# GRU and expert layer on one core: first expert products of steps 0 and 1 in column groups, six whole-array ones a block

## The chip, the cores and the metric

The kernel runs on one core of a Trainium2 chip. The metric is the device time of one execution in microseconds. Beside it stands one profiled execution, whose trace gives the start and the length of every instruction on TensorE (PE; its weight loads are listed apart as PEld), VectorE (DVE), ScalarE (ACT), GpSimd (POOL) and SyncE (SP, which issues the transfers).

## What is computed

A GRU runs over 256 time steps for 16 sequences of width 512, and its states go through a layer of eight low-rank experts, of which the two best of each state are mixed and added to the input:

```python
def cell(h, x):
    gi = x @ W_ih + b_ih
    gh = h @ W_hh + b_hh
    i_r, i_z, i_n = jnp.split(gi, 3, axis=-1)
    h_r, h_z, h_n = jnp.split(gh, 3, axis=-1)
    r = jax.nn.sigmoid(i_r + h_r)
    z = jax.nn.sigmoid(i_z + h_z)
    n = jnp.tanh(i_n + r * h_n)
    h_new = (1.0 - z) * n + z * h
    return (h_new, h_new)
...
    router_logits = x / norm @ router_w
    routing_weights = jax.nn.softmax(router_logits.astype(jnp.float32), axis=-1)
    rw, selected_experts = jax.lax.top_k(routing_weights, TOP_K)
    rw = rw / jnp.sum(rw, axis=-1, keepdims=True)
...
    for e in range(N_EXPERTS):
        out = out + combine[:, e, None] * (x @ Wa[e] @ Wb[e])
```

Here the layer's x is the GRU's states, `Wa[e]` is 512 x 128 and `Wb[e]` 128 x 512, and the whole function returns the input plus the layer's output.

## The kernel before

The recurrence is the backbone: step n needs the state of step n - 1. Eight steps make a block (S = 8; 8 steps x 16 sequences are 128 tokens), and there are 32 blocks (T = 256). Below, step s is n % 8. Every fp32 product is made of three fp16 ones (`TERMS`: high x high, high x low, low x high); a product whose stationary operand is still in the array skips its load (`matmul_held`, L843), others go by L852.

**TensorE.** A step begins with `state_part`: the state times the recurrent weights into the banks `gates` (L932 and L937) and `zbank`. These have 32 stationary columns and go to four column groups of the array, four matmuls side by side. The rest of a step is work that does not hang on the newest state:

- `pair_part`: the input products of two steps ahead into a bank `pairs`, in 12 units of four column-group matmuls with 384 moving columns. `UNITS` says how many an odd step does; the next even step does the rest.
- `expert_down`, the **first product** of expert e for a block: 12 matmuls with the whole array (128 stationary columns of `wa`, 128 tokens moving) into one of two `ybank`s.
- `expert_up_by_tokens`, the **second product**: three slots of four column-group matmuls (32 tokens stationary, 512 columns of `wb` moving) into `nbank` or `obank`.
- `route` in step 3: the router's logits of the block before, whole-array.

Expert e of block f has the number m = 8 f + e. `DOWN[e]` and `UP[e]` say how many steps after its block's first step the products are issued, so DOWN % 8 is the step's place in a block:

```python
DOWN = (9, 9, 11, 11, 13, 13, 15, 15)
UP = (12, 12, 14, 14, 16, 16, 18, 18)
UNITS = (12, 5, 12, 3, 12, 5, 12, 5)
...
for n in range(1, T):
    state_part(n)
    if n % 2:
        wide_step(n)
    else:
        grouped_step(n)
```

A wide step issues two first products (behind the router in step 3) and then its units; a grouped step its units and then two second products. The last twelve experts and the last block's first products are in `last_experts`.

**VectorE** carries the recurrence: it transposes `gates` (`tr`, L734), sums, makes `npre`, `u` and at last the new state `st` (L765), on which the next `gates` products wait. Behind that it does one `add_expert` a step (L801, expert m = n - 12) and in steps 0, 2, 5 and 6 a transpose of `gi_n` (L772). **ScalarE** does the sigmoids and the tanh, seeds `gates` and `zbank` from `pairs` (L570, L577), and in `beside` the rest: `split_y` (two copies of a first product, high part L645 and fp32 L649), `gather_states` for the router (L625, both halves in step 0), the bias copy, in the first 17 steps one weight split a step (L547). **GpSimd** subtracts to get a product's low part (`low_y`, L459) and does small things for the router. Both follow `downs_at`. SP's transfers are issued by step and none of them is touched.

Of the kernel before, what the change touches and what calls it, by code (L numbers as in the profile page):

```python
# [23 lines left out]
def wait(eng, sem, value):  # L24
    if value > 0:
        eng.wait_ge(sem, value)


def gru_moe_kernel(nc, x, cond, W_ih, W_hh, b_ih, b_hh, router_w, Wa, Wb, out):
# [4 lines left out]
    NB = T // S  # L34


    DOWN = (9, 9, 11, 11, 13, 13, 15, 15)
    UP = (12, 12, 14, 14, 16, 16, 18, 18)
    UNITS = (12, 5, 12, 3, 12, 5, 12, 5)
    ADD = S + 4  # L40
    YB = 6

# [10 lines left out]
    with ExitStack() as ctx:  # L53
# [106 lines left out]

        def downs_at(n):

            return [n - DOWN[e] + e for e in range(NE) if DOWN[e] % S == n % S and n >= DOWN[e]]

        def ups_at(n):
            return [n - UP[e] + e for e in range(NE) if UP[e] % S == n % S and n >= UP[e]]

# [3 lines left out]
        def y_at(m):  # L171
            return ybanks[m % 2]
# [228 lines left out]
        def _(pool):  # L401
# [100 lines left out]
            def beside(n):  # L502
                i, s = n // S, n % S
                if s == 0 and 1 <= i:
                    fold_squares(i - 1)
                    add_squares(i - 1)
                if s in (1, 2) and 1 <= i:
                    less_upper_half(i - 1, s - 1)
                if s == 3 and 1 <= i:
                    invert_norm(i - 1)  # L510
                if s == 4 and 1 <= i:
                    combine(i - 1)
                if s in (4, 6) and 1 <= i and i + 2 < NB:
                    split_x(i + 2, s // 6, n)
                for m in downs_at(n):
                    low_y(m)
                if s == 3 and 1 <= i:
                    gaps(i - 1)
# [19 lines left out]
        def _(act):  # L538
# [83 lines left out]
            def gather_states(f, part):  # L622
                act.wait_ge(both_parts_ready, 2 * ((f + 1) * S + 1))
                wait(act, logits_done, f)
                nc.scalar.activation(hf[:, part, :, :].rearrange("p k (s b) -> p (k s) b", b=B),  # L625
                                     hparts[:, f % HB, :, :, part * B:(part + 1) * B].rearrange(
                                         "p k s b -> p (k s) b"), ACT.Copy).then_inc(hf_ready, 1)
# [23 lines left out]
            def beside(n):  # L651
                i, s = n // S, n % S
                if s % 2 == 0 and n + 4 < T:
                    put_biases(n // 2 + 2)
                for m in downs_at(n):
                    split_y(m)
                if s == 7:
                    square(i)
                if s == 0 and 1 <= i:
                    for part in range(2):  # L660
                        gather_states(i - 1, part)
                if s == SPLIT_AT and i + 3 < NB:
                    split_x(i + 3)
                if s == SCALE_AT and 1 <= i and i + 2 < NB:
                    scale_x(i + 2)
                if n == 0:
                    split_first(2)
                if 0 <= n < len(SPLITS) - N_GRU_SPLITS:
                    split_weights(N_GRU_SPLITS + n)
# [170 lines left out]
        def _(pe):  # L840
# [8 lines left out]
            def product(held, out, lhsT, rhs, start, stop, cols=P, col0=0):  # L849
                if held:  # L850
                    return matmul_held(out, lhsT, rhs, cols, col0, start, stop)
                return nc.tensor.matmul(out, lhsT, rhs, start=start, stop=stop, skip_group_check=True)  # L852
# [96 lines left out]
            def route(f):  # L949
                bank = router_bank(f)  # L950

                if f == 0:
                    pe.wait_ge(weights_split, splits_before(N_RW_SPLITS))

                if f == NB - 1:
                    pe.wait_ge(acc_done, LEFT - 1)
                else:
                    pe.wait_ge(yhi_ready, f * NE + 2)
                    pe.wait_ge(y32_ready, f * NE + 2)

                wait(pe, router_read, f)
                pe.wait_ge(sq_step, (f + 1) * SQ_STEPS)
                for part in range(3):
                    nc.tensor.matmul(bank[:, P + NE:P + NE + 1], upper_half(part), ones_bf[:, :],
                                     start=(part == 0), stop=(part == 2), skip_group_check=True)
                pe.wait_ge(hf_ready, 2 * (f + 1))
                n = 0
                for k in range(K):
                    for ph, pw in TERMS:
                        mm = product((ph, pw) == (0, 1), bank[:, P:P + NE], hf[:, ph, k, :], rw[:, pw, k, :], n == 0,  # L970
                                     n == 3 * K - 1)
                        n += 1
                mm.then_inc(logits_done, 1)

            def wait_first_product(m):
                f, e = m // NE, m % NE

                wait(pe, yhi_ready, m - 1)
                wait(pe, y32_ready, m - 1)
                if e == 3 and f < NB - 1:  # L980
                    pe.wait_ge(router_read, f + 1)
                if e == 0:
                    pe.wait_ge(both_parts_ready, 2 * ((f + 1) * S + 1))
                if m in wa_split_at:
                    pe.wait_ge(weights_split, splits_before(wa_split_at[m]))

            def expert_down(m):
                f, e = m // NE, m % NE
                wait_first_product(m)
                n = 0  # L990
                for k in range(K):
                    for pw, ph in TERMS:
                        mm = product((pw, ph) == (0, 1), y_at(m)[:, 0:P], wa[:, pw, k, e, :],
                                     hparts[:, f % HB, k, :, ph * B:(ph + 1) * B], n == 0, n == 3 * K - 1)
                        n += 1
                mm.then_inc(y_done, 1)

# [36 lines left out]
            def pair_ahead(n):  # L1034

                s, p, all_units = n % S, (n + AHEAD) // 2, K * len(TERMS)
                if n % 2 and n > 1 and UNITS[s - 1] < all_units:
                    pair_part(p - 1, range(UNITS[s - 1], all_units))
                if p < T // 2:
                    pair_part(p, range(UNITS[s]) if n % 2 else range(UNITS[s - 1] if n else 6, UNITS[s] if n else all_units))  # L1040

# [7 lines left out]

            def grouped_step(n):  # L1050
                pair_ahead(n)
                for m in ups_at(n):
                    expert_up_by_tokens(m)
                if n == 0:
                    turn_first(2)

# [29 lines left out]
            grouped_step(0)  # L1086
            for n in range(1, T):
                state_part(n)
                if n % 2:
                    wide_step(n)  # L1090
                else:
                    grouped_step(n)
# [23 lines left out]
```

## Time and profile before

| what | value |
|---|---|
| median of 3 runs | 1017.51 us (1017.07 to 1017.79) |
| the profiled execution | 1017.07 us |
| its span, first to last instruction | 1015.3 us |
| PE busy | 979.9 us (97%) |
| DVE busy | 876.0 us (86%) |
| ACT busy | 694.6 us (68%) |
| POOL busy | 291.3 us (29%) |
| granted TensorE clock | 0.998 |

The span covers the execution but for 1.8 us around it. Matmuls of the four column groups overlap, so a slot of four counts once, and PE's busy time is that of a pipeline with modelled ends; what a slot costs is read from the distance between starts. A timeline row gives the start in us, the length, the engine, line and operation, the tile written and those read, the count of merged instructions, and in brackets the idle time before it and who ended it.

### The profile page before, as it was taken

How to read it: one execution, taken by the hardware profiler on the slowest of the kernel's cores; microseconds unless marked ns; L12 is line 12 of the kernel's file. 1: busy time of each engine (PE TensorE's matmuls, PEld its weight loads, DVE VectorE, ACT ScalarE, POOL GpSimd, SP SyncE). 2: the span in 40 equal slices, each digit the busy share in tenths (PEclk: the TensorE clock that was granted, in tenths of full speed). 3: DMA queues.
4: the chain of work that ended last, by engine and by line, in shares of the span. 5: the costliest groups of instructions: out<-in, count | busy, mean ns of one | idle time of the engine just before them, and what ended most of it. 6: DMA issues, size and time to landing. Idle time of an engine off the chain costs nothing.

```text
span 1015.3 us, 60728 instructions
## 1 busy us (share of the span) xinstructions
PE 979.9 (97%) x29067; PEld 669.2 (66%) x20799; DVE 876.0 (86%) x3631; ACT 694.6 (68%) x2696; POOL 291.3 (29%) x729
## 2 busy tenths in 40 slices
PE   4789999999999999999999999999999999999997
PEld 2456667667667666766667676676666676666664
DVE  6889888888888888888888888888888888888886
ACT  6687766776666677676677666667766667776663
POOL 1032323322323332322332233332223333223223
PEclk9999999999999999999999999999999999999999
DMA  8221111111111111111101111111111111110000
GB/s 301 87 81 31 29 32 30 30 28 33 27 32 33 28 26 35 27 32 32 30 24 35 30 30 30 32 26 32 29 29 33 30 24 33 30 30 19 15 9 28
DMA packets 49360, 38.83 MB, mean 38 GB/s; under 512 B 34532, under 2 KB 38972, under 8 KB 49084
## 3 DMA queue, kind: packets, MB, share of 16 engines
q1 hardware_dynamic: 48236, 31.41, 11.5%
q8 instruction: 198, 3.24, 1.4%
q10 hardware_dynamic: 848, 3.54, 1.0%
q14 instruction: 78, 0.64, 0.2%
HBM read 18.94 MB, written 8.39 MB: 27 GB/s over the span
## 4 chain that ended last, share of the span: by engine, by line
PE 89%; DVE 6%; ACT 2%; DMA 1%; issue 1%; ACTq 0%; DVEq 0%; POOL 0%; POOLq 0%
PE pairs L852 16%; PE ybank L852 12%; PE gates L932 11%; PE gates L937 11%; PE pairs L843 7%; PE ybank L843 6%; PE zbank L843 5%; PE zbank L852 5%; PE obank L852 5%; PE nbank L852 5%; PE obank L843 3%; PE nbank L843 2%; DMA wih<-in_L_cond_W_ih 1%; DVE acc L801 1%; DVE tr L734 1%
## 5 line engine op out<-in xcount | busy, mean ns | idle before, releaser
L852 PE MATMUL pairs<-wx,xs 128*32 128x384 f16 x4096 | 281.1, 328 | 1.2 <-DVE wx L714 1.2
L598 ACT ACTIVATE rr<-pre 128x64 f32<-128x64 f32 x256 | 65.7, 257 | 240.4 <-DVE pre L737 240.4
L852 PE MATMUL ybank<-hparts,wa 128*128 128x128 f16 x2048 | 193.9, 219 | 0.0
L459 POOL TENSOR_TENSOR y<-y 128x128 f16<-128x128 f32 x256 | 106.3, 436 | 258.8 <-ACT y L649 250.9
L852 PEld LDWEIGHTS ybank<-hparts,wa 128*128 128x128 f16 x2048 | 159.8, 98 | 29.5 <-issue 16.0
L843 PE MATMUL ybank<-hparts,wa 128*128 128x128 f16 x1024 | 178.2, 219 | 0.0
L843 PE MATMUL pairs<-wx,xs 128*32 128x384 f16 x2048 | 174.3, 326 | 0.0
L932 PE MATMUL gates<-whh,st 128*32 128x256 f16 x4080 | 157.3, 273 | 15.7 <-DVE st L765 15.5
L852 PEld LDWEIGHTS pairs<-wx,xs 128*32 128x32 f16 x4096 | 108.4, 97 | 95.9 <-issue 54.6
L932 PEld LDWEIGHTS gates<-whh,st 128*32 128x32 f16 x4080 | 103.5, 96 | 85.3 <-ACT gates L570 63.3
L937 PE MATMUL gates<-whh,hparts 128*32 128x256 f16 x4080 | 157.5, 273 | 0.0
L852 PE MATMUL zbank<-whh,hparts 128*32 128x128 f16 x4080 | 145.8, 219 | 0.0
L843 PE MATMUL zbank<-whh,hparts 128*32 128x128 f16 x4080 | 145.7, 219 | 0.0
L734 DVE STREAM_TRANSPOSE tr<-gates 128x256 f32<-128x256 f32 x256 | 114.6, 448 | 28.7 <-PE gates L937 20.7
L852 PEld LDWEIGHTS zbank<-whh,hparts 128*32 128x32 f16 x4080 | 114.3, 97 | 14.2
L937 PEld LDWEIGHTS gates<-whh,hparts 128*32 128x32 f16 x4080 | 111.9, 97 | 1.0
L570 ACT ACTIVATE gates<-pairs,step_rows 128x256 f32<-128x256 f32 x256 | 110.1, 430 | 0.1
L761 DVE SCALAR_TENSOR_TENSOR u<-nn,omz 128x64 f32<-128x64 f32 x256 | 57.7, 225 | 51.4 <-ACT nn L610 51.4
L606 ACT ACTIVATE zz<-pre 128x64 f32<-128x64 f32 x256 | 65.7, 257 | 50.8 <-DVE pre L745 47.2
L852 PE MATMUL obank<-wb,y 128*32 128x512 f16 (+1 forms) x980 | 98.2, 379 | 0.0
L852 PE MATMUL nbank<-wb,y 128*32 128x512 f16 x976 | 96.7, 379 | 0.0
L577 ACT ACTIVATE zbank<-pairs,step_rows 128x128 f32<-128x128 f32 x256 | 85.0, 332 | 0.0
(134 smaller groups left out, 1817.3 us busy)
## 6 DMA issues: line engine op xcount, KB each, us to landing
out<-outb SPq DMA_DIRECT2D x63, 128.0 KB
xin<-in_x SPq DMA_DIRECT2D x58, 128.0 KB
wih<-in_L_cond_W_ih ACTq DMA_DIRECT2D x4, 768.0 KB, 7.8
whh<-in_L_cond_W_hh SPq DMA_DIRECT2D x4, 768.0 KB, 12.0
wih<-in_L_ffn_Wb SPq DMA_DIRECT2D x8, 256.0 KB, 2.7
xs<-xh SPq DMA_TRANSPOSE x116, 3.0
wih<-in_L_ffn_Wa SPq DMA_DIRECT2D x4, 256.0 KB, 4.3
whh<-in_L_ffn_Wa SPq DMA_DIRECT2D x4, 256.0 KB, 3.0
```

What stands on the lines that cost most here:

```text
L459: nc.gpsimd.tensor_tensor(y[:, m % YB, 1, :], y32[:, m % 2, :], y[:, m % YB, 0, :], ALU.subtract).then_inc(ylo_ready, 1)
L570: nc.scalar.activation(gates[:, 0:2 * P], pairs[n // 2 % 2][:, 0:2 * P], ACT.Copy, scale=step_rows[:, q:q + 1]).then_inc(seeded, 1)
L577: nc.scalar.activation(zbank[:, 0:P], pairs[n // 2 % 2][:, 2 * P:3 * P], ACT.Copy, scale=step_rows[:, q:q + 1]).then_inc(z_seeded, 1)
L598: nc.scalar.activation(rr[:, :], pre[:, RG, :, :].rearrange("p k b -> p (k b)"), ACT.Sigmoid, scale=1 / PROD_SCALE).then_inc(r_ready, 1)
L606: nc.scalar.activation(zz[:, :, :].rearrange("p k b -> p (k b)"), zpre, ACT.Sigmoid, scale=1 / PROD_SCALE).then_inc(z_ready, 1)
L734: nc.vector.transpose(tr[:, 0:2 * K, :].rearrange("p (g k) c -> p g k c", k=K), gates[:, 0:2 * P].rearrange("p (g c k) -> p g k c", g=2, k ...
L761: nc.vector.scalar_tensor_tensor(out=u[:, :], in0=nn[:, :], scalar=PART_SCALE, in1=omz[:, :], op0=ALU.mult, op1=ALU.mult).then_inc(u_ready, 1)
L801: nc.vector.scalar_tensor_tensor(out=(outb if e == NE - 1 else acc)[:, :], in0=o_at(m)[:, :], scalar=comb[:, e:e + 1], in1=(xin[:, f % XIN ...
L843: return nc.tensor.add_instruction(mybir.InstMatmult(name=nc.get_next_instruction_name(), engine=mybir.EngineType.PE, start_tensor_calc=start,
L852: return nc.tensor.matmul(out, lhsT, rhs, start=start, stop=stop, skip_group_check=True)
L932: nc.tensor.matmul(gates[32 * j:32 * j + 32, 0:2 * P], st[:, k, :], whh[:, 1, k, j, 0:2 * P], start=False, stop=False, skip_group_check=True)
L937: mm = nc.tensor.matmul(gates[32 * j:32 * j + 32, 0:2 * P], prior[:, k, :], whh[:, 0, k, j, 0:2 * P], start=False, stop=(k == K - 1), skip ...
```

## The change

`DOWN` is now (11, 11, 13, 13, 15, 15, 16, 17): two first products each in steps 3, 5 and 7, and one each in steps 0 and 1 of the next block. `UP` has expert 5 a step later, so that steps 0 and 1 have one second product each. Step 1 is no wide step any more: steps 0 and 1 go through `grouped_step`, which issues the units, then a first product in column groups (`expert_down_by_ranks`: each of the 12 matmuls becomes four, with 32 of the 128 columns of `wa` each), then the second product. `UNITS` gives step 1 six units and step 2 the other six. Of the two gathers for the router one is in step 0 and one in step 1. GpSimd takes both low parts of steps 0 and 1 in step 1. For the last block's end, four first products are put into steps 254 and 255, whole-array.

```diff
-    DOWN = (9, 9, 11, 11, 13, 13, 15, 15)
-    UP = (12, 12, 14, 14, 16, 16, 18, 18)
-    UNITS = (12, 5, 12, 3, 12, 5, 12, 5)
+    DOWN = (11, 11, 13, 13, 15, 15, 16, 17)
+    UP = (12, 12, 14, 14, 16, 17, 18, 18)
+    UNITS = (12, 6, 12, 3, 12, 5, 12, 5)
...
         def downs_at(n):
 
+            if n >= T - 2:
+                return [LEFT + 2 * (n - T + 2), LEFT + 2 * (n - T + 2) + 1]
             return [n - DOWN[e] + e for e in range(NE) if DOWN[e] % S == n % S and n >= DOWN[e]]
...
-                for m in downs_at(n):
+                for m in (downs_at(n - 1) + downs_at(n) if s == 1 else [] if s == 0 else downs_at(n)):
                     low_y(m)
...
-                if s == 0 and 1 <= i:
-                    for part in range(2):
-                        gather_states(i - 1, part)
+                if s in (0, 1) and 1 <= i:
+                    gather_states(i - 1, s)
...
-                    pe.wait_ge(yhi_ready, f * NE + 2)
-                    pe.wait_ge(y32_ready, f * NE + 2)
+                    wait(pe, yhi_ready, f * NE)
+                    wait(pe, y32_ready, f * NE)
...
-                if e == 3 and f < NB - 1:
+                if e == 1 and f < NB - 1:
                     pe.wait_ge(router_read, f + 1)
...
+            def expert_down_by_ranks(m):
+                f, e = m // NE, m % NE
+                wait_first_product(m)
+                n = 0
+                for k in range(K):
+                    for pw, ph in TERMS:
+                        for g in range(4):
+                            of = slice(32 * g, 32 * g + 32)
+                            mm = product((pw, ph) == (0, 1), y_at(m)[of, 0:P], wa[:, pw, k, e, of],
+                                         hparts[:, f % HB, k, :, ph * B:(ph + 1) * B], n == 0, n == 3 * K - 1, 32, 32 * g)
+                        n += 1
+                mm.then_inc(y_done, 1)
...
             def grouped_step(n):
                 pair_ahead(n)
+                if n < T - 2:
+                    for m in downs_at(n):
+                        expert_down_by_ranks(m)
                 for m in ups_at(n):
                     expert_up_by_tokens(m)
+                if n == T - 2:
+                    for m in downs_at(n):
+                        expert_down(m)
...
-                if n % 2:
+                if n % S in (3, 5, 7):
                     wide_step(n)
```

TensorE, step 0 of a steady block, from its first input units (`pairs`) to its end; `ybank` rows are first products, `nbank` and `obank` rows second ones. Before:

```order
L852 MATMUL pairs<-wx,xs 32x384 x8
L843 MATMUL pairs<-wx,xs 32x384 x4
L852 MATMUL pairs<-wx,xs 32x384 x8
L843 MATMUL pairs<-wx,xs 32x384 x4
L852 MATMUL pairs<-wx,xs 32x384 x4
L852 MATMUL nbank<-wb,y 32x512 x4
L843 MATMUL nbank<-wb,y 32x512 x4
L852 MATMUL nbank<-wb,y 32x512 x4
L852 MATMUL obank<-wb,y 32x512 x4
L843 MATMUL obank<-wb,y 32x512 x4
L852 MATMUL obank<-wb,y 32x512 x4
```

And now, from the last input unit on:

```order
L853 MATMUL pairs<-wx,xs 32x384 x4
L853 MATMUL ybank<-hparts,wa 32x128 x4
L844 MATMUL ybank<-hparts,wa 32x128 x4
L853 MATMUL ybank<-hparts,wa 32x128 x8
L844 MATMUL ybank<-hparts,wa 32x128 x4
L853 MATMUL ybank<-hparts,wa 32x128 x8
L844 MATMUL ybank<-hparts,wa 32x128 x4
L853 MATMUL ybank<-hparts,wa 32x128 x8
L844 MATMUL ybank<-hparts,wa 32x128 x4
L853 MATMUL ybank<-hparts,wa 32x128 x4
L853 MATMUL nbank<-wb,y 32x512 x4
L844 MATMUL nbank<-wb,y 32x512 x4
```

The second of the two second products has left the step, and 48 matmuls of a grouped first product have come between the units and the other one.

TensorE, step 1 of a steady block, from the last `zbank` slot to the first units. Before, there are 24 whole-array matmuls between them:

```order
L843 MATMUL zbank<-whh,hparts 32x128 x4
L852 MATMUL ybank<-hparts,wa 128x128
L843 MATMUL ybank<-hparts,wa 128x128
L852 MATMUL ybank<-hparts,wa 128x128 x2
L843 MATMUL ybank<-hparts,wa 128x128
```

Now the units come first, and the step stays in column groups to its end:

```order
L844 MATMUL zbank<-whh,hparts 32x128 x4
L853 MATMUL pairs<-wx,xs 32x384 x4
L844 MATMUL pairs<-wx,xs 32x384 x4
L853 MATMUL pairs<-wx,xs 32x384 x8
L844 MATMUL pairs<-wx,xs 32x384 x4
L853 MATMUL pairs<-wx,xs 32x384 x4
L853 MATMUL ybank<-hparts,wa 32x128 x4
L844 MATMUL ybank<-hparts,wa 32x128 x4
```

Six units stand where five stood behind the whole-array products, and the first product is a grouped one behind them.

## Rows read from the trace of the kernel before

**Rows 1.** The page: shares of the chain; a group of loads (busy us, mean ns)

```profile
PE 89%; DVE 6%; ACT 2%; DMA 1%; issue 1%; ACTq 0%; DVEq 0%; POOL 0%; POOLq 0%
...
L852 PEld LDWEIGHTS pairs<-wx,xs 128*32 128x32 f16 x4096 | 108.4, 97 | 95.9 <-issue 54.6
```

**Rows 2.** Timeline of PE, steps 0 to 2 of a steady block: start us, length us, what

```profile
572.81 0.62 PE L932 MATMUL gates<-whh,st 128*32 128x256 f16 x16
...
574.13 0.51 PE L852 MATMUL pairs<-wx,xs 128*32 128x384 f16 x8
...
575.27 0.40 PE L852 MATMUL nbank<-wb,y 128*32 128x512 f16 x4
...
576.56 0.62 PE L932 MATMUL gates<-whh,st 128*32 128x256 f16 x16
...
577.44 0.24 PE L852 MATMUL zbank<-whh,hparts 128*32 128x128 f16 x4
...
577.83 0.24 PE L843 MATMUL zbank<-whh,hparts 128*32 128x128 f16 x4
578.00 0.23 PE L852 MATMUL ybank<-hparts,wa 128*128 128x128 f16 x1
...
579.30 0.22 PE L852 MATMUL ybank<-hparts,wa 128*128 128x128 f16 x1
579.45 0.35 PE L852 MATMUL pairs<-wx,xs 128*32 128x384 f16 x4
...
580.11 0.34 PE L843 MATMUL pairs<-wx,xs 128*32 128x384 f16 x4
580.30 0.62 PE L932 MATMUL gates<-whh,st 128*32 128x256 f16 x16
...
584.05 0.41 PE L932 MATMUL gates<-whh,st 128*32 128x256 f16 x8
```

**Rows 3.** Timeline of PE, first block: starts of steps 2, 3 and 4

```profile
32.98 0.62 PE L932 MATMUL gates<-whh,st 128*32 128x256 f16 x16 [1.40 <-DVE st L765]
...
36.63 0.62 PE L932 MATMUL gates<-whh,st 128*32 128x256 f16 x16 [1.01 <-DVE st L765]
...
40.35 0.62 PE L932 MATMUL gates<-whh,st 128*32 128x256 f16 x16 [1.73 <-DVE st L765]
```

**Rows 4.** Timeline of PE, last block: starts of steps 254 and 255

```profile
989.52 0.62 PE L932 MATMUL gates<-whh,st 128*32 128x256 f16 x16 [0.70 <-DVE st L765]
...
993.23 0.62 PE L932 MATMUL gates<-whh,st 128*32 128x256 f16 x16 [0.92 <-DVE st L765]
```

**Rows 5.** Timeline of DVE, the stretch of rows 2: tr, st, one expert add

```profile
573.92 0.45 DVE L734 STREAM_TRANSPOSE tr<-gates 128x256 f32<-128x256 f32 x1 [0.19 <-PE gates L937]
...
576.09 0.23 DVE L765 TENSOR_TENSOR st<-u,v 128x64 f16<-128x64 f32 x1
...
576.86 0.71 DVE L801 SCALAR_TENSOR_TENSOR acc<-nbank,comb,acc 128x512 f32<-128x512 f32 x1
577.67 0.45 DVE L734 STREAM_TRANSPOSE tr<-gates 128x256 f32<-128x256 f32 x1
...
579.92 0.23 DVE L765 TENSOR_TENSOR st<-u,v 128x64 f16<-128x64 f32 x1
```

**Rows 6.** Timeline of PEld (weight loads), the same stretch

```profile
577.33 0.51 PEld L852 LDWEIGHTS zbank<-whh,hparts 128*32 128x32 f16 x16
...
581.56 0.18 PEld L852 LDWEIGHTS pairs<-wx,xs 128*32 128x32 f16 x8
```

**Rows 7.** Timelines of PE and ACT, steps 8 and 9

```profile
58.73 0.62 PE L932 MATMUL gates<-whh,st 128*32 128x256 f16 x16 [1.00 <-DVE st L765]
...
62.60 0.62 PE L932 MATMUL gates<-whh,st 128*32 128x256 f16 x16
...
59.20 1.13 ACT L625 ACTIVATE hf<-hparts 128x512 f16<-128x512 f16 x2
```

**Rows 8.** Timeline of POOL, the low parts of step 7's first products

```profile
573.42 0.82 POOL L459 TENSOR_TENSOR y<-y 128x128 f16<-128x128 f32 x2 [3.28 <-ACT y L649]
```

## Prediction

> **What bounds the kernel now.** I read first the shares of the chain that ended last, for the whole execution, then TensorE's timeline over three steps of a steady block, then VectorE's over the same stretch, then stretches in which TensorE has too little to do. TensorE holds 89% of it [rows 1], but that hides two different kinds of step. A step begins with its first `gates` product. Steps 0, 1 and 2 of this block begin at 572.81, 576.56 and 580.30, and step 3 at 584.05 [rows 2]: 3.75, 3.74 and 3.75 us. In step 0 the last expert product runs straight into the next `gates` (1.32 us of state products, seven input units in 1.14 us, so 0.163 each, six groups of second products in 1.29 us, so 0.215 each): TensorE sets that step. In step 1 the last unit starts at 580.11 and would be through at 580.27, yet `gates` starts at 580.30: there the recurrence sets the end, by 0.03 us.
>
> How fast the recurrence can go is seen where TensorE idles. In the first block, which has no experts, steps 2 and 3 take 36.63 - 32.98 = 3.65 and 40.35 - 36.63 = 3.72 us, with idle times of about a microsecond and more before `gates`, each released by VectorE's `st` [rows 3]. Near the end, with VectorE adding experts as usual, step 254 takes 993.23 - 989.52 = 3.71 us [rows 4]. VectorE's rows give the pieces [rows 5]: `gates` begins about 1.1 us ahead of `tr` (576.56 to 577.67), `tr` to `st` takes 576.09 - 573.92 = 2.17 us in step 0 and 579.92 - 577.67 = 2.25 in step 1 (the odd step has one more semaphore wait in it), and the next `gates` starts 0.38 after `st` when it is waited for. So no even step can be under about 3.65 us, no odd one under about 3.72. Step 5 escapes the extra wait, and nothing is changed there.
>
> **The transitions.** In step 1 the last of the column-group products (`zbank`) starts at 577.83; groups of that kind start 0.056 apart ((577.83 - 577.44) / 7), yet the first whole-array product starts at 578.00, 0.17 later. The last whole-array one starts at 579.30 and the column groups go on at 579.45, 0.15 later [rows 2]. Against 0.056 that is 0.11 and 0.09 lost; with slower first intervals on each side a whole-array stage costs 0.22 to 0.24 us beside its products. There are four such stages in a block, and three after the change.
>
> **The change, part by part.** The array time of a first product does not change by itself. Whole, 24 matmuls for two experts take 24 slots of 0.056, 1.34 us. In column groups one expert is 12 slots of four matmuls with 128 moving columns, the shape of the `zbank` slots, which also take 0.056: 12 x 0.056 = 0.67 us. This form with `wa` is not in the trace. Its lower bound is these 0.67 us (the moving columns are the same number, so nothing makes it less). Its upper bound is from the loads: the `zbank` slots come with 16 weight loads in 8 slots, 0.445 us, or 27.8 ns a load; a grouped first product has 32 loads in 12 slots, and if 27.8 ns were the pace of a load it would take 0.89 us. I take 0.67, because elsewhere eight loads of the same 32-column form are together over in 0.18 us, though one lasts 97 ns by itself [rows 1, 6]: they overlap across the column groups and start 10 ns apart or closer, while 0.67 / 32 = 21 ns is needed.
>
> The Trainium skill speaks against that choice. "TensorE: Matmul & The Clock Gate", section on LDWEIGHTS, gives a load's time as its columns divided by 1.2 ns, which for 32 columns is 26.7 ns, and "TensorEngine Tiling (Array Packing)", Gotcha 2, says that column tiling excludes fast weight load. An estimate by these pages, with the loads one behind the other, is 0.85 us a product, and the sum below would come out near 1022.5 us.
>
> The steps then need of TensorE:
> - Step 0: 1.32 + 1.14 + 0.67 + one second product 0.645 = 3.78 us (was 3.75). TensorE sets it.
> - Step 1: 1.32 + six units 0.98 + 0.67 + 0.645 = 3.61. The recurrence needs 3.72, so it takes 3.72 (was 3.74), with TensorE idle for 0.11.
> - Step 2: 1.32 + 0.98 + 1.29 = 3.59. The recurrence needs 3.65 (was 3.75), idle 0.06.
> - Steps 3 to 7 issue the same on TensorE: two whole-array first products in 3, 5 and 7, two second products in 4 and 6.
>
> Together 11.15 us against 11.24 in this block [rows 2], and against 11.23 by the middle of all 29 blocks: about 0.08 a block. That is the point of the sum: of the 0.22 us and more taken off TensorE two thirds turn into waiting for `st`. Steps 0 to 2 of the blocks 3 to 31 are of this kind, 29 x 0.08 = **2.3 us gained**.
>
> At the start, step 9 takes 62.60 - 58.73 = 3.87 where 3.72 is possible. ScalarE gathers both halves of `hf` (1.13 us) ahead of a weight split in step 8 and comes late to the next sigmoid [rows 7]. The change puts one half into step 9, and takes the first products and their copies out of it; step 10 loses their low parts beside its own sums. I put twice the 0.15 us of step 9, **0.3 us gained**, between 0 and 0.35. In steps 13 to 18 VectorE carries weight splits and expert adds together; nothing of that moves, 0.
>
> At the end, step 254 now has two whole-array first products behind its two second products: 1.32 + 1.29 + 1.34 + about 0.2 of transitions = 4.15 to 4.17, where the recurrence took 3.71 [rows 4]. **0.45 us lost**, and nothing later gets it back, since everything that follows hangs on the last state.
>
> Costs put at nothing. The two y copies of an expert move on ScalarE (two from step 1 to step 0, one gather the other way); both steps leave it idle before the next sigmoid. The two GpSimd subtractions stay in step 1. The lead of a second product over its first shrinks from three steps to one, but a pair whose first products were in step 7 has its low parts by 573.42 + 0.82 = 574.24 us [rows 8], and an even step asks for the first of them 2.46 us into itself (575.27 in step 0 [rows 2]), a microsecond later; only step 4 has its first products 0.4 us later in the step before, behind the router, and it asks 0.33 us later too. The last second product of step 0 now ends with the step: a slot lasts 0.40 us and the next starts 0.215 after it, so its end is 0.18 after the next `gates` starts; VectorE's add starts 0.3 after it (576.86 against 576.56 [rows 2, 5]), so the margin is a few hundredths to a tenth. If that cover fails the add slips by as much, and has 0.1 us more before `tr`. No DMA moves.
>
> Sum: -2.3 - 0.3 + 0.45 = -2.15 us. The profiled execution took 1017.07 us against a median of 1017.51; taken off the median this gives **1015.3 us**. A measurement of this kernel can tell about 0.2% (2.0 us) from no change, and the forecast stands right on that edge.
>
> **The rivals.**
> - *The loads set the pace* (slower than before). At 27.8 ns a load the product takes 0.89 us; step 0 becomes 4.00, step 1 3.83, step 2 stays at 3.65: 11.48, 0.24 more than before, x 29 = +7.0, and with start and end 1024.6 us. It turns the sign from about 0.75 us a product, since step 1 hides 0.11 us but step 0 nothing. For it: exactly 27 to 28 ns a load is what `zbank` and `gates` slots have. Against: the eight loads in 0.18 us [rows 6]. The skill's rule is this rival, at 1022.5. Chance 0.13.
> - *The gain drowns.* Some 0.04 to 0.08 us a block are lost in step 0 (a bubble where the grouped product meets its semaphores) or in step 2, which has no slack at all any more, so that any lateness of VectorE counts there: 29 x 0.08 gone leaves +0.15, 1016.5 to 1018 us. Chance 0.22.
> - *The recurrence is no floor here.* Then the whole 0.22 to 0.24 us a block comes through, less the 0.45 at the end: 29 x 0.23 = 6.7, so 1017.51 - 6.7 - 0.3 + 0.45 = 1011.0 us; with half of it 1014.3. Against it: the 0.03 us of idle already seen in step 1. Chance 0.15.
>
> **How the numbers follow.** The forecast has 0.50, with 1014.3 to 1016.4 as its own range; some six tenths of it lie beyond 0.2%. Faster: 0.30 + 0.15 and a little of the second rival, 0.46. Within 0.2%: 0.39. Slower: 0.15. The range leaves out the deepest part of the third rival and the full price of the first: 1013 to 1020 us.
>
> **What would show it.** Right: steps 0, 1 and 2 of a steady block of 3.78, 3.72 and 3.65 us; twelve slots of `ybank` in 0.67 us with no jump at either side; idle time before `gates` put down to `st` of 0.11 us after step 1 and 0.06 after step 2, in all some 5 us more than before; step 254 at 4.15. Wrong: slots of `ybank` over 0.062 us, a `gates` in step 2 that starts later than 0.38 after `st`, or a VectorE add that waits for TensorE.

## The result and the profile after

| | before | after |
|---|---|---|
| median, 12 runs each on one chip | 1017.28 us (1016.47 to 1017.96) | 1019.18 us (1018.64 to 1020.68) |
| profiled execution: time, span | 1017.07, 1015.3 us | 1019.46, 1017.7 us |

The ratio is 1.0019, with an interval of 1.0012 to 1.0027: the change costs about 1.9 us, where 2.15 us of gain were forecast. The lines of the page that differ, first of the kernel before:

```profile
PE 979.9 (97%) x29067; PEld 669.2 (66%) x20799; DVE 876.0 (86%) x3631; ACT 694.6 (68%) x2696; POOL 291.3 (29%) x729
...
q8 instruction: 198, 3.24, 1.4%
```

and of the changed kernel:

```profile
PE 980.1 (96%) x31227; PEld 676.3 (66%) x22239; DVE 876.5 (86%) x3631; ACT 695.6 (68%) x2696; POOL 291.6 (29%) x729
...
q8 instruction: 212, 3.47, 1.4%
PE 89%; DVE 6%; ACT 2%; DMA 1%; issue 1%; ACTq 0%; DVEq 0%; POOL 0%; POOLq 0%
```

TensorE is busy for as long as before, and the chain has the shares of [rows 1], though the span is 2.4 us longer. What changed are the counts: 2160 matmuls and 1440 loads more (60 grouped products by 36 and 24). The queue that brings instructions carried 14 more packets of 16 KB, and 3600 / 256 = 14.06. TensorE's semaphore instructions count too: with the some 960 that each trace records it has 50830 instructions before and 54429 after, and divided by 256 that is 198.6 and 212.6, for 198 and 212 packets. A packet is 256 TensorE instructions, in every run below as well.

The three steps that the prediction rested on, in the stretch that answers to [rows 2]; timeline of PE in the changed kernel, start and length in us:

```profile
574.44 0.62 PE L933 MATMUL gates<-whh,st 128*32 128x256 f16 x16
...
576.73 0.35 PE L853 MATMUL pairs<-wx,xs 128*32 128x384 f16 x4
576.89 0.24 PE L853 MATMUL ybank<-hparts,wa 128*32 128x128 f16 x4
...
577.51 0.24 PE L853 MATMUL ybank<-hparts,wa 128*32 128x128 f16 x4
577.56 0.40 PE L853 MATMUL nbank<-wb,y 128*32 128x512 f16 x4
...
578.21 0.62 PE L933 MATMUL gates<-whh,st 128*32 128x256 f16 x16
...
581.94 0.62 PE L933 MATMUL gates<-whh,st 128*32 128x256 f16 x16
```

Step 0 takes 578.21 - 574.44 = 3.77 us and step 1 takes 3.73. The twelve `ybank` slots take 577.56 - 576.89 = 0.67 us, with no jump at either side. From the starts of `gates` in blocks 3 to 30 the middle lengths of steps 0, 1 and 2 are 3.772, 3.731 and 3.651 us (before 3.749, 3.731 and 3.749), and steps 3 to 7 are as they were. That is 0.075 us a block gained, as forecast. Step 24 starts at 118.37 (before 118.56), 0.19 gained. The gain is there in nearly every block, and yet the kernel is slower.

The rest is in single steps. Adding up by how much each step from 24 to 252 exceeds the middle length of its place in the block gives 1.7 us before and 6.0 us after. In the kernel before these are nearly all five VectorE operations that start some 0.35 us late, in steps 48, 63, 178, 193 and 239; the other kernels have them too (e4 all but the one in step 48). The new ones are on TensorE. Timeline of PE around one in step 57:

```profile
244.24 0.40 PE L853 MATMUL nbank<-wb,y 128*32 128x512 f16 x4
244.46 0.41 PE L933 MATMUL gates<-whh,st 128*32 128x256 f16 x8
245.42 0.40 PE L933 MATMUL gates<-whh,st 128*32 128x256 f16 x8 [0.56 <-issue]
245.63 0.62 PE L938 MATMUL gates<-whh,hparts 128*32 128x256 f16 x16
```

PEld over the same stretch:

```profile
244.31 0.36 PEld L933 LDWEIGHTS gates<-whh,st 128*32 128x32 f16 x9 [0.16 <-ACT gates L572]
245.42 0.12 PEld L933 LDWEIGHTS gates<-whh,st 128*32 128x32 f16 x7 [0.76 <-issue]
```

Matmuls and loads stop together in the middle of `gates`, where nothing waits on a semaphore, and the idle time is put down to "issue": to nothing that the profile shows. The ninth matmul starts 0.83 us after the eighth, 0.74 later than its place in the row of slots, and step 57 is longer by 0.74 us. The waits of the whole execution show it: before, `tr` waited for `gates` 93 times, 20.7 us in all and 0.4 at the longest; after,

```profile
DVE tr L735 <- PE gates L938: 24.5, 96, 1.1
```

There are seven such stops between steps 24 and 252, of 0.33 to 1.01 us in steps 34, 43, 57, 105, 162, 209 and 233, with one of 0.29 in step 81 and smaller ones beside them. The eight together are 4.3 us, which is what the excess has grown by. Numbering all of TensorE's records in the trace from 0 (matmuls, loads and its semaphore instructions, in the order of their starts), **every one of the seven stands ahead of a record whose number leaves 193 when divided by 256**. The transfers around the stop in step 57 (from 242.0 to 244.2 us):

```profile
q1 hardware_dynamic: 230, 0.05, 11.6%
q8 instruction: 1, 0.02, 4.8%
```

4.8% of 16 engines over 2.2 us is one packet of 1.69 us. By the list of transfers it started at 242.31 and ended at 244.00, and the next instruction ran at 245.42, 1.42 later. For the six others of these stops the distance from the packet's end to the next instruction is 1.4 to 1.7 us. So the theory taken into the experiments, **F**: TensorE reaches the end of its 256 instructions before the next 256 are there, because with a grouped first product (80 instructions for 0.67 us of work, where a whole-array one has 20) a step has some 260 instructions instead of 200. Its rivals: **W**, the stops are waits for other engines that the new order brings; **L**, the grouped loads are slow somewhere; **C**, only the number of packets counts, however they are spread.

### The profile page after: what moved, and what is told of

Read it like the earlier page. It is cut to its first block, busy times and chain, and to the rows that moved or that the text cites. A ratio compares the mean times of both kernels' runs of the same rounds, so it can differ in the third digit from the quotient of the medians.

```text
span 1017.7 us, 64327 instructions
## 1 busy us (share of the span) xinstructions
PE 980.1 (96%) x31227; PEld 676.3 (66%) x22239; DVE 876.5 (86%) x3631; ACT 695.6 (68%) x2696; POOL 291.6 (29%) x729
## 3 DMA queue, kind: packets, MB, share of 16 engines
q8 instruction: 212, 3.47, 1.4%
## 4 chain that ended last, share of the span: by engine, by line
PE 89%; DVE 6%; ACT 2%; DMA 1%; issue 1%; ACTq 0%; DVEq 0%; POOL 0%; POOLq 0%
PE pairs L853 16%; PE ybank L853 12%; PE gates L933 12%; PE gates L938 11%; PE pairs L844 7%; PE ybank L844 6%; PE zbank L853 5%; PE zbank L844 5%; PE obank L853 5%; PE nbank L853 5%; PE nbank L844 2%; PE obank L844 2%; DMA wih<-in_L_cond_W_ih 1%; DVE tr L735 1%; DVE acc L802 1%
## 5 line engine op out<-in xcount | busy, mean ns | idle before, releaser
L853 PE MATMUL pairs<-wx,xs 128*32 128x384 f16 x4096 | 287.3, 328 | 0.9 <-DVE wx L715 0.9
L853 PE MATMUL ybank<-hparts,wa 128*32 128x128 f16 (+1 forms) x3488 | 200.0, 219 | 0.0
L853 PEld LDWEIGHTS ybank<-hparts,wa 128*32 128x32 f16 (+1 forms) x3488 | 167.1, 97 | 30.9 <-issue 12.0
L844 PE MATMUL ybank<-hparts,wa 128*128 128x128 f16 (+1 forms) x1744 | 181.2, 219 | 0.4 <-issue 0.4
L844 PE MATMUL pairs<-wx,xs 128*32 128x384 f16 x2048 | 176.4, 327 | 0.0
L853 PEld LDWEIGHTS pairs<-wx,xs 128*32 128x32 f16 x4096 | 113.1, 97 | 95.1 <-issue 53.6
L933 PE MATMUL gates<-whh,st 128*32 128x256 f16 x4080 | 158.5, 273 | 16.9 <-DVE st L766 16.1
```

Source lines behind the costliest of these rows:

```text
L844: return nc.tensor.add_instruction(mybir.InstMatmult(name=nc.get_next_instruction_name(), engine=mybir.EngineType.PE, start_tensor_calc=start,
L933: nc.tensor.matmul(gates[32 * j:32 * j + 32, 0:2 * P], st[:, k, :], whh[:, 1, k, j, 0:2 * P], start=False, stop=False, skip_group_check=True)
```

## Experiments

**e1_quarter: the changed kernel without three quarters of the grouped products.** It leaves out ranks 32 to 127 of experts 6 and 7 in blocks 0 to 29, so its time is that of less work.

```diff
-                        for g in range(4):
+                        for g in range(1):
```

> The changed kernel, but a grouped first product issues only the matmuls of its first column group: 12 matmuls and 8 loads instead of 48 and 32, the same 12 slots of array time, the same mode, the same waits. It leaves out ranks 32 to 127 of experts 6 and 7 (4 to 7's last blocks aside). Theory F (the steady steps got faster as forecast, but the denser instruction stream of steps 0 and 1 outruns TensorE's instruction fetch at some of the 256-instruction boundaries): the pauses before instructions number 193 + 256 k go, the middle step lengths stay at 3.77, 3.73 and 3.65, and the time is about 4 us under the changed kernel, near 1015 us, below the kernel before. Rival W (the pauses are waits for other engines, which the new places of the products bring): the waits are the same, so the time stays at 1019 us. Rival L (weight loads set the pace somewhere): it would fall too, but the slots of ybank would get shorter than 0.056 us.

Measured: 1015.32 us, ratio 0.9983 (0.9974 to 0.9992). The page:

```profile
PE 977.9 (97%) x29067; PEld 676.7 (67%) x20799; DVE 874.9 (86%) x3631; ACT 695.0 (69%) x2696; POOL 294.8 (29%) x729
...
q8 instruction: 198, 3.24, 1.3%
```

The count of matmuls and loads is exactly that of before, the packets too, and of the stops one of 0.30 us is left; excess over middle lengths 2.1 us. Single steps did not come as expected (steps 0 and 1 take 3.654 and 3.838: three of the four matmuls of the second product's first slot start some 0.2 us ahead of the first product's last one, which shortens step 0, and in step 1 VectorE's add comes late and puts off `tr` by 0.11), but steps 0 to 2 together take 11.14 against 11.15 in the changed kernel. With the same gain and without the stops it is 1.65 us faster than the kernel before measured beside it (1016.97 us), where 2.15 were forecast; that its time is the forecast 1015.3 to the digit is chance. It takes loads away too, so by itself it does not tell F from L.

**e2_dense_before: the kernel before with more instructions for the same columns.** In steps 0 and 1 every unit is cut in three matmuls of 128 columns, the second and third with their weights held: 56 and 40 instructions more.

```diff
+                    for c in (range(3) if cut else (None,)):
+                        to, of = (slice(P, 4 * P), slice(0, 3 * P)) if c is None else (
+                            slice((c + 1) * P, (c + 2) * P), slice(c * P, (c + 1) * P))
```

> The kernel before, with nothing moved, but from step 24 on each 384-column matmul of the input units of steps 0 and 1 is cut into three of 128 columns with the same weights held: 56 more instructions in step 0 and 40 in step 1, no load more. Array time by slots of 0.056 against 0.163: 0.005 us a unit, 0.03 a block that counts, 1.0 to 1.2 us in all. Theory F: pauses appear at instruction boundaries as in the changed kernel, 2 to 5 us on top, so 1020 to 1023 us. Rival W: no pauses, 1018.3 us.

Measured: 1019.82 us, ratio 1.0025 (1.0014 to 1.0036), between W's 1018.3 and F's 1020 to 1023; q8 has 209 packets (2784 / 256 = 10.9 more). It is slower, with no grouped product, no load and no wait added. Only part is F's: stops at the 193rd record are 0.48 us in step 226 and 0.25 in step 148; the middle length of step 0 grew by 0.035 (1 us in all); and in this execution the first step began 0.58 us later. So a small weight for F by itself, against W and L.

**e3_padded: the changed kernel with 64 idle matmuls and their loads ahead of everything.**

```diff
+            for _ in range(64):
+                nc.tensor.matmul(gates[:, 0:P], zeros, zeros, start=True, stop=True, skip_group_check=True)
```

> The changed kernel with 64 idle matmuls and their 64 loads ahead of everything else on TensorE, while it would wait for the first transfers: 128 instructions, half a block of 256. Theory F: the pauses stay at numbers 193 + 256 k of the instructions as recorded and so move to other steps; their sum is of the same size, 3 to 6 us, and the time within 2 us of 1019. Rival W: the pauses stay in the same steps as in the changed kernel (34, 43, 57, 81, 105, 162, 233) and move away from 193 + 256 k to 65 + 256 k.

Measured: 1018.66 us, ratio 1.0017 (1.0006 to 1.0027), excess 6.1 us, as large as without the shift. (The profiled execution is the longest of the ten, 1022.08 us; its first step began 2.7 us later than the changed kernel's.) No step of the changed kernel's list has its stop again: step 57 runs through, and the long stops are now in steps 41, 121, 145, 146, 169, 211, 235 and 250 (0.26 to 0.86 us). All eight stand again ahead of records that leave 193. The first of them, timeline of PE:

```profile
188.01 0.24 PE L853 MATMUL ybank<-hparts,wa 128*32 128x128 f16 x4
188.06 0.40 PE L853 MATMUL obank<-wb,y 128*32 128x512 f16 x3
188.86 0.39 PE L853 MATMUL obank<-wb,y 128*32 128x512 f16 x1 [0.40 <-issue]
```

The stop cuts a slot of four matmuls after the third. A wait of the program would move with the step; this one stays at a count of instructions. That is the clearest evidence for F, and it excludes W; L has no place for it either, since no load of the steps was changed.

**e4_halves: the grouped product in two groups of 64 columns**, 24 matmuls and 16 loads.

```diff
-                        for g in range(4):
-                            of = slice(32 * g, 32 * g + 32)
+                        for g in range(2):
+                            of = slice(64 * g, 64 * g + 64)
```

> The changed kernel with a grouped first product in two groups of 64 columns: 24 matmuls and 16 loads instead of 48 and 32. If column groups of 64 stand beside those of 32 without a transition, the array time is the same, half of the added instructions are gone and with them the pauses: 1015 to 1016 us. If 64 columns are a mode of their own, each such product pays 0.2 us of transitions as a whole-array stage does: step 0 becomes 3.99 and step 1 3.83, 0.33 us a block more, so 1019.2 - 4 + 9.6 = 1025 us.

Measured: 1025.86 us, ratio 1.0085 (1.0072 to 1.0099). No stop is left (excess 2.0 us, 203 packets), but steps 0 and 1 take 4.020 and 3.847. Timeline of PE, step 0:

```profile
579.18 0.35 PE L853 MATMUL pairs<-wx,xs 128*32 128x384 f16 x4
579.46 0.25 PE L853 MATMUL ybank<-hparts,wa 128*64 128x128 f16 x2
...
580.10 0.22 PE L853 MATMUL ybank<-hparts,wa 128*64 128x128 f16 x2
580.25 0.40 PE L853 MATMUL nbank<-wb,y 128*32 128x512 f16 x4
```

After a unit the next slot of the same form comes 0.163 later, here 0.28; and behind the product 0.15 in place of 0.056. Groups of 64 columns beside groups of 32 pay about what a whole-array stage pays. So fewer instructions took the stops away, and the transitions cost more than the stops had.

**e5_spread: the grouped products in steps 0 and 2, with step 1 sparse between them.** `DOWN` and `UP` are changed, the end is as in the kernel before.

```diff
+    DOWN = (8, 10, 11, 11, 13, 13, 15, 15)
+    UP = (12, 12, 14, 14, 16, 17, 17, 18)
```

> Same number of grouped first products and of transitions as in the changed kernel, but the two dense steps stand apart: DOWN = (8, 10, 11, 11, 13, 13, 15, 15), so the grouped ones are in steps 0 and 2, UP = (12, 12, 14, 14, 16, 17, 17, 18), so step 1 has two second products, and nothing is added at the end. Steps 0, 1 and 2: 3.78, 3.73 and 3.65, 0.07 a block less than before, 2.0 us, and 0.2 at the start. Theory F with the density within one block of 256 instructions as what decides: a fetch boundary now seldom finds a full block in a dense stretch, the pauses shrink to 1 us or less, and the time is 1015 to 1016.5 us, under both kernels. If instead only the number of instructions counts, it is 1018 to 1019 us.

Measured: 1021.5 us, ratio 1.005 (1.0036 to 1.0064), excess 7.6 us, middle lengths 3.772, 3.729, 3.649: a miss. A sparse step between two dense ones does not help. The longest stop, in step 138 at the 193rd record, is in the middle of a slot of the grouped product:

```profile
554.28 0.22 PE L842 MATMUL ybank<-hparts,wa 128*32 128x128 f16 x1
555.09 0.22 PE L842 MATMUL ybank<-hparts,wa 128*32 128x128 f16 x3 [0.60 <-issue]
```

A step of 260 instructions is longer than a packet: one that falls within it is used up in the step alone, whatever its neighbour does. That covers six of this kernel's ten stops over 0.25 us. The other four, the longest among them, ended packets that took 4.3 to 4.6 us; what sets them apart is told below the table.

**e6_both_in_1: both grouped products in step 1**, which then has 312 instructions (112 + 40 + 160; the recorded text has 304) (`DOWN` and `UP` of the kernel before, six units).

```diff
+    DOWN = (9, 9, 11, 11, 13, 13, 15, 15)
+    UP = (12, 12, 14, 14, 16, 16, 18, 18)
```

> DOWN and UP of the kernel before, but the two first products of step 1 are grouped ones, with six units in steps 1 and 2 each: 304 instructions in step 1. Medians: step 0 3.75, step 1 3.72 (needs 3.64), step 2 3.65: 0.10 a block, 2.9 us less than before, no cost at the end. Theory F: this is the densest stream of all, 256 instructions in about 2.7 us, so pauses are longer, 0.5 us and more wherever a boundary falls there, and eat the gain: 1017 to 1021 us. Rival W: 1014 us.

Measured: 1025.6 us, ratio 1.0087 (1.0073 to 1.01), worse than expected. Middle lengths hardly move (3.749, 3.735, 3.669), and the excess is 15.5 us: 24 stops of 0.3 to 1.0 us, all at the 193rd record. The profiled execution is the longest of the five. The waits of this kernel:

```profile
DVE tr L733 <- PE gates L936: 31.9, 92, 1.2
```

The count of packets is 213, as in e5 and e8 below, and the excess twice theirs: C falls, how fast a packet is used up does count.

**e7_units5: the changed kernel with five units in step 1 and seven in step 2**, to see whether the state sets the length of steps 1 and 2.

```diff
-    UNITS = (12, 6, 12, 3, 12, 5, 12, 5)
+    UNITS = (12, 5, 12, 3, 12, 5, 12, 5)
```

> The changed kernel with five units in step 1 and seven in step 2. If the recurrence is the floor as forecast, step 1 stays at 3.73 though TensorE has 0.16 us less to do, and step 2 goes from 3.65 to 3.75, so 0.10 a block, 2.9 us more, with somewhat fewer pauses: 1020 to 1022 us. If there is no such floor the two steps together stay at 7.38 and the time at 1019 us.

Measured: 1021.22 us, ratio 1.0042 (1.0028 to 1.0056). Timeline of PE, steps 1 and 2:

```profile
578.84 0.62 PE L933 MATMUL gates<-whh,st 128*32 128x256 f16 x16
...
582.57 0.62 PE L933 MATMUL gates<-whh,st 128*32 128x256 f16 x16
...
586.32 0.62 PE L933 MATMUL gates<-whh,st 128*32 128x256 f16 x16
```

Step 1 keeps its 3.73 us with 0.163 us less to do; step 2, which has that unit more, goes from 3.65 to 3.75. So the recurrence is the floor of step 1, and step 2 had 0.06 us above TensorE's need.

**e8_tail: the changed kernel with step 254's two first products in column groups.**

```diff
-                if n < T - 2:
-                    for m in downs_at(n):
-                        expert_down_by_ranks(m)
+                for m in downs_at(n):
+                    expert_down_by_ranks(m)
...
-                if n == T - 2:
-                    for m in downs_at(n):
-                        expert_down(m)
```

> The changed kernel with the two first products of step 254 grouped instead of whole-array. Step 254 becomes 1.32 + 1.29 + 1.34 = 3.95 instead of 4.15: 0.2 us less, which the times can't tell from nothing; the trace can.

Measured: 1019.37 us, ratio 1.0022 (1.0013 to 1.0031). Step 254 takes 3.95 in place of 4.18, the transitions' 0.22. The program is otherwise that of the changed kernel, and the stops are mostly in its steps again (34, 57, 105, 162, 209 and 233 among them) with other lengths (step 57 1.10, step 105 0.88): the places are fixed by the program, the lengths vary from execution to execution. The excess is 7.2 us (steps 24 to 252 alone), against 6.0 in the changed kernel with the same instructions there: that much can differ between two executions.

**e9_woven and e10_bunched: the changed kernel's instructions of steps 0 and 1 in other orders.** By then F was held in a sharper form: what counts is how fast the last 190 or so instructions ahead of the end of a packet run. Both kernels have the same instructions a step; one weaves slots of units (U), the grouped first product (Y) and the second product (P), the other puts the first product right ahead of the next `gates`.

```diff
+    ORDER = {0: "UYYYUUYYUYPPYYYUUYYYUP", 1: "UUUYYUUYYYYPPYYUPYYYY"}
```

```diff
+    ORDER = {0: "UUUUUUUPPPYYYYYYYYYYYY", 1: "UUUUUUPPPYYYYYYYYYYYY"}
```

> The changed kernel with the same instructions in steps 0 and 1 in another order (blocks 3 to 30): units, slots of the grouped first product and slots of the second product take turns, so that the 80 short instructions of the first product are spread over the step. Counts, tile forms and step lengths stay. Theory F (pauses come where TensorE runs through the some 190 instructions ahead of a 256 boundary faster than a block is fetched): the fastest 190 consecutive records of the changed kernel take 2.33 us; here by slot lengths 2.6 us. Steps 0, 1, 2 keep their middle lengths of 3.77, 3.73 and 3.65; the excess over middle lengths falls from 6.0 to 2.5 to 4.5 us; time 1016.0 to 1018.0 us. Theory C (only the number of fetched blocks counts, 212 as in the changed kernel): excess near 6, 1019.2 us. If the turns between banks cost something by themselves, step 0 gets longer than 3.80 and time goes above 1020.

> The changed kernel with the same instructions in steps 0 and 1, but units first, then the second product, then the grouped first product right ahead of the next gates (blocks 3 to 30). The 80 short instructions then stand against the 112 of gates and zbank: by slot lengths the fastest 190 consecutive records take 2.0 us in place of 2.33. Theory F: more and longer pauses, excess 8 to 13 us, time 1021 to 1026 us, middle lengths as in the changed kernel. Theory C (number of fetched blocks, unchanged): 1019.2 us.

Measured: 1019.15 us, ratio 1.002 (1.0011 to 1.0029), excess 5.6 us; and 1018.91 us, ratio 1.0018 (1.0009 to 1.0027), excess 5.1 us. Both miss. In e9 the weaving brought the fastest 190 records from 2.33 to 2.43 us only, not to 2.6, so it is a weak test; in e10 they take 1.90, and neither the time nor the excess went up. Even the stop of step 57 stays where it was. Timeline of PE of e10, where other work stands ahead of it:

```profile
243.59 0.24 PE L854 MATMUL ybank<-hparts,wa 128*32 128x128 f16 x4
243.65 0.41 PE L934 MATMUL gates<-whh,st 128*32 128x256 f16 x8
244.47 0.40 PE L934 MATMUL gates<-whh,st 128*32 128x256 f16 x8 [0.42 <-issue]
```

More telling is the time in which a whole packet is used up, from one 193rd record to the last one ahead of the next (stretches between 118.5 and 985 us, one execution of each kernel; stops counted behind stretches of every length; excess as above; a stop of 0.25 to 0.3 can be mostly the usual wait for the state):

| kernel | packets (q8) | fastest stretch of 256, us | stretches under 4.0 us | stops over 0.25 us at a 193rd record | excess, us |
|---|---|---|---|---|---|
| before | 198 | 4.26 | 0 | 0 | 1.7 |
| e4_halves | 203 | 4.19 | 0 | 0 | 2.0 |
| e1_quarter | 198 | 4.21 | 0 | 1 | 2.1 |
| e2_dense_before | 209 | 3.51 | 27 | 1 | 3.2 |
| e7_units5 | 212 | 3.48 | 51 | 6 | 4.0 |
| e10_bunched | 212 | 3.60 | 52 | 8 | 5.1 |
| e9_woven | 212 | 3.50 | 51 | 7 | 5.6 |
| after | 212 | 3.49 | 51 | 8 | 6.0 |
| e3_padded | 213 | 3.49 | 52 | 8 | 6.1 |
| e8_tail | 213 | 3.48 | 51 | 12 | 7.2 |
| e5_spread | 213 | 3.47 | 47 | 10 | 7.6 |
| e6_both_in_1 | 213 | 2.58 | 31 (26 under 3.5) | 24 | 15.5 |

A step of 3.73 us with some 256 instructions uses a packet up in a step however they are ordered, which fits that e9 and e10 changed nothing, and e5 nothing for the better.

The length of the stretch alone does not decide it. The list of transfers, taken together with the records, does. The twelve traces have 2240 such stretches and 85 stops. Where the next packet's transfer ended 1.5 us or more ahead of the last record of the packet in use (2072 times), there is no stop; where it ended less than 1.1 us ahead of it (67 times), there is one 66 times. From the end of a transfer to the first record of its packet it is never under 1.15 us, and 1.2 to 1.8 at the stops. No transfer began more than 0.8 us ahead of the first record of the packet before it. So a stop is what three times have over the stretch: from the previous 193rd record to the start of the transfer, the transfer itself, and about 1.4 us behind it. Of the 85 stops 17 ended stretches of 4.0 to 5.4 us, and there the transfer had begun 1.6 to 3.7 us after the previous 193rd record; the longest of e5 is one (3.19 us late in a stretch of 4.58).

## Why the prediction was wrong

- *The transitions, the grouped product, the steps.* Right. The first product takes 0.67 us in groups; steps 0, 1 and 2 take 3.77, 3.73 and 3.65 (forecast 3.78, 3.72, 3.65); e4 shows the transition once more as 0.1 us on each side. Over 29 blocks 2.2 us came in. One sign did not show where it was looked for: TensorE's waits on `st` are 16.1 us in all, against 15.5 before, not some 5 us more, because a row of 0.40 us reaches over so short a gap. The starts show it: from the last slot to the next `gates` it is 0.31 us after step 1 and 0.26 after step 2, where a slot takes 0.215, so 0.10 and 0.04 us idle against 0.11 and 0.06 forecast.
- *The floor.* Right: e7 moved a unit and step 1 stayed at 3.73. The rival without a floor is out.
- *The loads set the pace.* Out. 32 loads in 0.67 us are 21 ns each. (The eight loads of [rows 6] start 11 ns apart in the mean, not 10 or closer, which changes nothing.) The Trainium skill's time of a load in "TensorE: Matmul & The Clock Gate", section on LDWEIGHTS, taken for one load behind the other, would give 0.85 us; this trace does not agree, with loads that take turns over four column groups.
- *The start.* The sign right, the size off: 0.19 us gained where 0.3 was put. Step 9 came down from 3.87 to 3.82 only, step 10 from 3.93 to 3.78.
- *The end.* Right: step 254 takes 995.60 - 991.42 = 4.18 us (forecast 4.15 to 4.17; 3.71 before), 0.46 us lost.
- ***Costs put at nothing.*** **This is the step that failed.** It went through copies, subtractions, semaphores and transfers of the program, and "No DMA moves" was true of those alone. The 60 instructions that a grouped product has beside a whole-array one were counted as array time and as loads, never as instructions that have to be brought. What the runs showed in its place is that TensorE stops for 0.3 to 1.0 us where a packet of 256 instructions is used up before the next is there. That put 4.3 us on the account (6.0 less 1.7): -2.2 - 0.2 + 0.46 + 4.3 = 2.36, against 2.4 between the two spans (1.9 between the medians).
- *The rivals.* "The gain drowns" had the right form, a bubble in dense steps, but was priced at no more than the gain, and as a small loss in each block. It is none in most blocks and half a microsecond or more in a few. The only rival on the slower side was the one on loads. The range of 1013 to 1020 still holds the measured time, but by luck: it was drawn for other rivals than the one that came.

The Trainium skill has the mechanism and speaks against its mattering: "Runtime: NRT & Kernel Launch", section "Instruction fetch mechanics", says that instructions come in blocks of 16 KB, 256 of them, fetched while the block before runs, at a cost that is "mostly hidden". The q8 counts agree with the first part. The second holds for the kernel before, where no stretch of 256 goes under 4.26 us, and not for the changed one, with 51 under 4.0.

What stays open: what sets the start of a packet's transfer. Over the changed kernel it starts between 0.5 us ahead of the previous 193rd record and 3.1 us behind it (0.64 behind in the middle), at its eight stops 0.95 us or more behind it in each case; what holds it up in those cases was not tried. So the number of stretches under 4 us does not give the excess (e2 has 27 of them and 1 stop, e7 51 and 6).

No kernel beats both: the only one below the kernel before is e1, which leaves work out.

## What to carry to other kernels

Before a product is cut into narrower tiles, count the instructions of the engine, loads included, for every stretch of 256 of them, and compare the time in which they run with that of the densest stretch that the kernel has now. Here the three kernels that never went under 4.19 us had one stop between them. Of the other nine eight had 6 to 24 each, and e2, with 27 stretches under 4.0 us where most have some 50, had one. No length was safe or lost by itself: 24 of the 38 stretches under 3.5 us ended without a stop over 0.25 us, and 17 stretches of 4.0 us or more ended with one. A gap put down to "issue" that cuts through a group of matmuls and recurs at the same remainder of the instruction number is the mark of it, and a few idle instructions at the start of the program, which shift all numbers, tell it from a wait. Reordering inside the stretch did not cure it here (e9, e10). Fewer instructions did (e1, e4), though e1 leaves work out and e4 paid more for its transitions than the stops had cost.

## What the runs showed of the hardware

- TensorE's instructions came in packets of 16 KB, one for each 256 matmuls, loads and semaphore instructions: 198, 203, 209, 212 and 213 packets for 50830, 52029, 53614, 54429 and 54550 recorded instructions (before, e4, e2, after, e5). A packet took 0.88 to 2.1 us, and the first instruction of it ran 1.2 to 1.8 us after its end where TensorE was waiting for it.
- In 2240 packets the transfer never began more than 0.8 us ahead of the first instruction of the packet before: each packet was fetched only about when the one ahead of it came into use, or later.
- Weight loads of 32 columns go at 21 ns each when they alternate over the four column groups, with no slot longer than 0.056 us for it.
- A column group of 64 beside groups of 32 costs 0.12 us more ahead of its first slot and 0.1 behind its last; products in groups of 32 follow one another for nothing (0.67 us for twelve slots, no jump at either side).
- Two profiled programs that differ only in step 254 (the changed kernel and e8) had their long stops mostly in the same steps, with other lengths (step 105: 0.33 and 0.88 us). The spread of the times was 1.5 us in 12 runs before, 2.0 in 12 after and 5.2 in 10 runs of e3; how much of the last is the stops, and how much a later first step, was not separated.
